# A vision tower on one core: four edits to its patch stage and to the place of two small matrices' powers

## The chip, the cores and the metric

The kernel runs on one core of one Trainium2 chip. The metric is the device time of one execution in microseconds (us). Three runs of the kernel before took 324.05, 324.23 and 325.01 us: median 324.23. Engines: PE is TensorE, DVE VectorE, ACT ScalarE, POOL GpSimd, SP SyncE. Transfers are issued on two queues here, SyncE's (q1 in the profile) and ScalarE's (q10), and run on the core's 16 DMA engines.

## The reference, cut to what matters

Sixteen images of 3 x 96 x 96 become 36 patches of 768 numbers each; with the class token an image has 37 tokens of 256, 592 in all. Two layers follow: attention and a mixture of experts, then an iterated attention with 16 x 16 matrices `Wlq`, `Wlk`, `Wlv` and a quantised feed-forward. The change touches the patch stage:

```
patches = x.reshape(B, C, h, P, w, P).transpose(0, 2, 4, 3, 5, 1).reshape(B, h*w, P*P*C)
y = layernorm(patches) * ln1_w + ln1_b
y = einsum('bnp,pd->bnd', y, lin_w) + lin_b
y = layernorm(y) * ln2_w + ln2_b
y = concatenate([cls_token, y], axis=1) + pos_embedding[:, :n + 1]
```

and, in the second layer's attention, in three iterations, `ql = qcur @ Wlq.T + blq`, `kl = kcur @ Wlk.T + blk`, `vl = vcur @ Wlv.T + blv` on every head, with `kcur, vcur = kl, vl` and `qcur` raised by each output. The kernel puts products of these small matrices (their powers) into the projections once.

## The kernel before, in words

Everything is fp32 and stays in the on-chip memory. Tokens lie in five tiles of 128 rows (`TT = 5`, the last of 80). The program of each engine is written out by hand, in order; engines wait for each other by semaphores. TensorE's eight banks are handed out in rotation in the order of one list, `fills()`: the n-th fill waits until the (n-8)-th has been emptied by the engine named beside it, and all engines count through the same list (`fill`, `full`, `take`, `empty`, `emptied`).

The patch stage, in TensorE's order:

- `ln`: after six matmuls on constants (`keep_awake`) TensorE transposes the rows of `ln1_w` and `ln1_b` (`ln_rows`, L1712); ScalarE copies them to `ln_cols` (L694).
- `ad`: `table` has 37 rows, the position embedding and seven selector columns. VectorE (`make_table`, L1015 to L1026) waits for three transfers (L663 to L665: positions, class token and `ln2_b`, the last two broadcast to 37 rows), adds the class token to row 0 and the bias to the others, and fills the selectors. Five products with `token_all` (for each of 640 token rows a 1 in the row of its position, made by GpSimd at L569) give the addend of every token; ScalarE copies them (L697).
- `channel(c)`: GpSimd (L579) and ScalarE (L684) copy the windows of an image's channel into patches, TensorE transposes them (L1729), ScalarE writes `patT` (L691).
- `cs`: the column sums of `lin_w` weighted by `ln1_w` and `ln1_b`, four chains of six products with `lin_w` as the stationary side and 2 moving columns; then `mr` and `cr`, the sums as rows on all partitions by transposes of a broadcast column (L1744). ScalarE makes `mean_row` (L703).
- VectorE computes the channel statistics from the images (L1068) and centres the six chunks of `lin_w` with `ln_cols` and `mean_row` (`centred_weights`, L1072), chunks 0 to 3 before the statistics of channel 2, 4 and 5 after the aggregates (L1083); then `c_row` (L1090), which empties the bank of `cr`.
- `y`: the embedding of tiles 0 and 1, chunk by chunk (L1775), after `channel(2)`; then the rates `rt`, tiles 2, 3 and 4. VectorE applies the second normalisation and adds the addend (L1125 to L1148).

Then `small_matrices`, the turned weights of the first attention, and `pw`, two fills of three products (`powers`), which ScalarE copies to `wlT` (L716); `turn` transposes the normalised tokens xn (L1840) into `xT` (L740) for the projections (L1865). The powers' users, `composed_weights` (`wc`), come on TensorE after the first attention, near 111 us; ScalarE scales and copies them (L720), in its order `q`, 1, 2, then the root of the variances for the next layer norm (L672), then 3. SyncE's queue issues the images (L480), `lin_w` (L483) and some thirty further transfers without waiting.

Of the kernel before, what the change touches and what calls it, by code (L numbers as in the profile page):

```python
# [84 lines left out]
POOL_WINDOWS = 4  # L85

# [3 lines left out]
def fills():  # L90
# [4 lines left out]
    f = [(("ln",), "act")]  # L95
    f.extend((("ad", t), "act") for t in range(TT))
# [15 lines left out]
    f.extend((("pw", n), "act") for n in range(2))  # L112
# [15 lines left out]
    f.extend((("wc", n), "act") for n in ("q", 1, 2, 3))  # L128
# [76 lines left out]
def build(nc, i, out):  # L205

    with ExitStack() as ctx:
# [89 lines left out]
        col_sums = cut(cur, 4)  # L297
# [18 lines left out]
        r_lin, r_ln2w, r_ln2b = (sqr_all[:, n * D:(n + 1) * D] for n in range(3))  # L316
        rsd_all = sb("rsd", P, NR * CF)
        rsd = rsd_all[:, :].rearrange("p (n t) -> p n t", n=NR)
        token_all = rsd_all[0:T, 0:NP]
        token_of = rsd_all[0:T, 0:NT].rearrange("p (b t) -> p b t", t=T)  # L320
# [4 lines left out]
        table = probs_all[0:T, 0:DA]  # L325
        r_cls = probs_all[0:T, 2 * D:3 * D]
# [80 lines left out]
        weights_centred = sem("weights_centred")  # L407
        attn_cleared = sem("attn_cleared")
# [123 lines left out]
        def _(pool):  # L532
# [35 lines left out]
            link(pool.memset(token_all[:, NT:NP], 0.0))  # L568
            pool.tensor_copy(token_of, ident[0:T, 0:T].unsqueeze(1).to_broadcast([T, B, T])).then_inc(consts_ready, 1)  # L569
# [78 lines left out]
        def _(act):  # L648
# [44 lines left out]
            b = take(act, ("ln",))  # L693
            empty(act.copy(ln_cols.rearrange("p c v k -> p (c v k)"), b[:, 0:4 * NC]))  # L694
            for t in range(TT):
                b = take(act, ("ad", t))
                empty(act.copy(addend[:, t, :], b[:, 0:DA]))  # L697
            windows(0)
            channel(0)
            b = take(act, ("cs",))  # L700
            empty(act.copy(col_sums, b[:, 0:4]))
# [44 lines left out]
            for n in range(2):  # L746
                powers(n)
# [57 lines left out]
            for n in ("q", 1, 2):  # L805
                composed_weights(n)
# [174 lines left out]
        def _(dve):  # L981
# [33 lines left out]
            def make_table():  # L1015

                dve.wait_ge(pos_in, 48)
                dve.tensor_reduce(table[:, D + 1:DA], ident[0:T, 1:T].rearrange("p (g w) -> p w g", g=NG), AX.X, ALU.add)  # L1018
                dve.tensor_scalar(first[:, 1:2], ident[0:T, 0:1], -1.0, 1.0, ALU.mult, ALU.add)
                link(dve.tensor_copy(first[:, 0:1], ident[0:T, 0:1]))  # L1020
                link(dve.scalar_tensor_tensor(out=table[:, 0:D], in0=r_cls, scalar=first[:, 0:1], in1=table[:, 0:D],
                                              op0=ALU.mult, op1=ALU.add))
                dve.tensor_copy(table[:, D:D + 1], first[:, 1:2])
                link(dve.scalar_tensor_tensor(out=table[:, 0:D], in0=r_ln2b[0:T, :], scalar=first[:, 1:2],
# [54 lines left out]
            for k in range(4):  # L1079
                centred_weights(k)  # L1080
# [1158 lines left out]
```

## Time and profile before

| | |
|---|---|
| median of three runs | 324.23 us |
| profiled execution, its own time | 322.2 us |
| its span | 320.5 us |
| TensorE busy | 264.7 us (83%), 2221 matmuls |
| VectorE busy | 201.6 us (63%) |
| ScalarE busy | 100.4 us (31%) |
| GpSimd busy | 45.0 us (14%) |

The span is what the views divide; the rest of the execution's time lies around it. Busy matmul time overlaps, since matmuls are pipelined. In the page's picture of 40 slices of 8 us, TensorE's row begins 403969: busy 40% of the first slice, under 10% of the second, 30% of the third, then 90% or more with one slice of 60%. The row PEclk gives the granted clock in tenths, 9 for nine tenths or more.

### The profile page before, as it was taken

Reading aid. Unit: us, or ns where it says so; the run is one execution under the profiler, and the core shown is the slowest. Engines: PE = TensorE matmul, PEld = TensorE weight load, DVE = VectorE, ACT = ScalarE, POOL = GpSimd, SP = SyncE. Lnnn points to the kernel's source line nnn. Section 1 sums busy time; section 2 is a strip of 40 time slices with the busy share of each in tenths; the row PEclk is TensorE's granted clock in tenths of the full one; section 3 lists DMA queues with packets and bytes.
Section 4 is the critical chain, followed back from the end, with each engine's and each line's share of the span. In section 5 each row is a group of like instructions: output and inputs, shape, how many; then the busy total and the mean of one; then the engine's idle time right before and its main releaser. Section 6 shows DMA issues by size and latency. Waiting matters only on the chain.

```text
span 320.5 us, 5617 instructions
## 1 busy us (share of the span) xinstructions
PE 264.7 (83%) x2221; PEld 218.8 (68%) x2221; DVE 201.6 (63%) x485; ACT 100.4 (31%) x238; POOL 45.0 (14%) x88
## 2 busy tenths in 40 slices
PE   4039699678987989999999998998868899937496
PEld 3028688578977757777787798876646677717484
DVE  1051608953683536889788962786788846997931
ACT  1004610333224154211111253476330533917000
POOL 7140000020053000000000000679400000000000
PEclk9999979879557999999999986999999999987789
DMA  7919500500000043000000000000000000000011
GB/s 205 221 22 314 169 2 1 164 3 2 4 0 2 4 149 146 2 0 0 0 2 1 0 2 1 2 3 0 4 0 3 0 0 2 0 0 0 1 35 43
DMA packets 14524, 12.10 MB, mean 38 GB/s; under 512 B 2975, under 2 KB 13954, under 8 KB 14498
## 3 DMA queue, kind: packets, MB, share of 16 engines
q1 hardware_dynamic: 14376, 11.62, 12.3%
q8 instruction: 18, 0.29, 0.4%
q10 hardware_dynamic: 122, 0.12, 0.1%
q14 instruction: 8, 0.07, 0.1%
HBM read 11.13 MB, written 0.61 MB: 37 GB/s over the span
## 4 chain that ended last, share of the span: by engine, by line
PE 66%; DVE 18%; ACT 6%; DMA 5%; issue 3%; ACTq 1%; DVEq 0%
PE bank L1702 47%; DMA sqr<-in_L_tok_ln_b 5%; PE bank L2206 5%; PE bank L1865 3%; PE bank L1898 2%; DVE part L1546 2%; PE bank L1775 2%; PE bank L1929 2%; DVE big L1610 1%; DVE keys_n L1591 1%; PE bank L1840 1%; PE bank L1973 1%; DVE big L1644 1%; ACT xT L740 1%; PE bank L1729 1%
## 5 line engine op out<-in xcount | busy, mean ns | idle before, releaser
L1702 PE MATMUL bank<-xT,big 128*128 128x296 f32 (+1 forms) x192 | 45.7, 391 | 0.0
L1702 PEld LDWEIGHTS bank<-xT,big 128*128 128x128 f32 x192 | 34.3, 190 | 9.5 <-issue 0.2
L1702 PE MATMUL bank<-xT,fT 128*128 128x296 f32 (+12 forms) x96 | 24.6, 416 | 0.6 <-DVE xT L1567 0.6
L1702 PE MATMUL bank<-big,cur 128*128 128x256 f32 (+1 forms) x100 | 23.3, 381 | 0.7 <-DVE cur L1321 0.7
L822 ACT ACTIVATE cen<-bank 128x296 f32<-128x296 f32 x20 | 8.3, 418 | 46.4 <-PE bank L1702 40.7
L1697 PE MATMUL bank<-ident,ones 128*128 128x128 f32 x100 | 17.1, 340 | 6.2 <-POOL rsd L569 4.4
L1702 PEld LDWEIGHTS bank<-xT,fT 128*128 128x128 f32 x96 | 17.2, 191 | 7.1 <-issue 2.1
L1702 PEld LDWEIGHTS bank<-big,cur 128*128 128x128 f32 (+1 forms) x100 | 18.0, 182 | 4.9 <-DVE cur L1321 1.5
L1697 PEld LDWEIGHTS bank<-ident,ones 128*128 128x128 f32 x100 | 16.4, 253 | 6.6 <-POOL rsd L569 4.4
L1334 DVE SCALAR_TENSOR_TENSOR h<-bank,route,h 128x256 f32<-128x256 f32 (+1 forms) x40 | 17.0, 478 | 2.8 <-PE bank L1702 2.8
L624 POOL TENSOR_SCALAR big<-keys_n,k_w 128x256 f32<-128x256 f32 x24 | 17.5, 750 | 6.4 <-DVE keys_n L1425 6.4
L1546 DVE TENSOR_REDUCE part<-big 128x1 f32<-128x296 f32 (+2 forms) x18 | 13.1, 731 | 6.3 <-ACT big L958 6.3
L1702 PE MATMUL bank<-probs,rsd 37*128 37x263 f32 x10 | 4.7, 658 | 13.4 <-DVE first L1026 13.4
L2206 PE MATMUL bank<-fT,big 128*128 128x256 f32 (+1 forms) x60 | 15.2, 419 | 0.6 <-DVE big L1543 0.6
L2206 PEld LDWEIGHTS bank<-fT,big 128*128 128x128 f32 (+1 forms) x60 | 12.2, 206 | 3.4 <-DVE big L1543 0.8
L1702 PEld LDWEIGHTS bank<-probs,rsd 37*128 37x128 f32 x10 | 3.2, 327 | 14.4 <-DVE first L1026 13.5
L616 POOL COPY cur<-xT 128x256 f32<-128x256 f32 x2 | 0.8, 404 | 80.9 <-ACT xT L742 80.9
L1321 DVE TENSOR_TENSOR cur<-cen,bank 128x296 f32<-128x296 f32 x20 | 9.1, 461 | 4.8 <-PE bank L1702 4.4
L1702 PE MATMUL bank<-wT_o,att 128*128 128x256 f32 (+1 forms) x40 | 9.3, 383 | 1.5 <-DVE att L1502 0.9
L606 POOL TENSOR_TENSOR big<-big,row_sum 128x370 f32<-128x370 f32 x8 | 6.2, 813 | 24.8 <-DVE row_sum L1217 24.8
L1702 PEld LDWEIGHTS bank<-wT_o,att 128*128 128x128 f32 (+1 forms) x40 | 7.0, 182 | 3.1 <-DVE att L1502 1.3
L1018 DVE TENSOR_REDUCE probs<-ident 37x6 f32<-37x36 f32 x1 | 0.2, 208 | 14.2 <-DMA sqr<-in_L_tok_ln_b 14.2
(312 smaller groups left out, 540.2 us busy)
## 6 DMA issues: line engine op xcount, KB each, us to landing
big<-in_x SPq DMA_DIRECT2D x3, 576.0 KB, 11.8
big<-in_L_ffn_w_gate SPq DMA_DIRECT2D x2, 512.0 KB, 6.5
big<-in_L_ffn_w_up SPq DMA_DIRECT2D x2, 512.0 KB, 6.7
big<-in_L_ffn_w_down SPq DMA_DIRECT2D x1, 1024.0 KB, 5.5
small<-in_L_tok_lin_w SPq DMA_DIRECT2D x3, 256.0 KB, 5.5
small<-in_L_ffn_w_gate SPq DMA_DIRECT2D x1, 768.0 KB, 4.6
small<-in_L_ffn_w_up SPq DMA_DIRECT2D x1, 768.0 KB, 6.8
small<-in_L_ffn_w_down SPq DMA_DIRECT2D x1, 768.0 KB, 8.1
```

The source lines that it names most:

```text
L624: ins = pool.tensor_scalar(fkeys[a - 1][:, u, :, n, :], keys, k_w[:, a - 1, n:n + 1], 1.0, ALU.mult, ALU.mult)
L822: empty(act.activation(silu[:, c, :], b[:, 0:HP], ACT.Silu))
L1321: empty(dve.tensor_tensor(hid[:, e % 3, c * HP:(c + 1) * HP], silu[:, c, :], b[:, 0:HP], ALU.mult))
L1334: ins = dve.scalar_tensor_tensor(out=v, in0=src, scalar=route[0:n, t, e:e + 1], in1=v, op0=ALU.mult, op1=ALU.add)
L1546: return dve.tensor_reduce(part[:, n:n + 1], v, AX.X, ALU.max, apply_absolute_value=True)
L1697: pe.matmul(b[:, 0:P], ones[:, :], ident[:, :], start=True, stop=True)
L1702: ins = pe.matmul(out_, a_, b_, start=(n == 0), stop=(n == len(pairs) - 1))
L1775: ins = pe.matmul(bs_[t][:, 0:D], patT[:, k, t * P:(t + 1) * P], lin_w[:, k, :], start=(k == 0), stop=(k == PK - 1))
L1865: ins = pe.matmul(b[32 * j:32 * j + m, at_:at_ + 4 * T].rearrange("p (u c) -> p u c", u=2), w(k), xq[:, k, :, 2 * j * T:2 * (j + 1) * T], ...
L1898: ins = pe.matmul(bs_[j][:, (2 * t + s) * T:(2 * t + s + 1) * T], qT[rows, row:row + P], kT[rows, u, s * T:(s + 1) * T], start=True, stop= ...
L1929: ins = pe.matmul(b[32 * q:32 * q + 32, m * 2 * T:(m + 1) * 2 * T].rearrange("p (i t) -> p i t", i=2), vals[0:G3, 3 * u + g, s, h_, :], by ...
L2206: ins = pe.matmul(b[0:rows, 0:D], gate[:, o * NT + t * P:o * NT + t * P + rows], fT[2][:, o, :], start=(o == 0), stop=(o == FC - 1))
```

## The change

- ScalarE's first transfers: the positions in 32 rows and 5 rows, the class token and `ln2_b` as one row each, all to `table`, which now has 39 rows (`TR = T + 2`); then the two of `ln1`. The broadcasts are gone.
- GpSimd builds `token_all` with 39 rows: token 0 of an image selects row 0 and row 37, the others their position and row 38. So the products add class token and bias. `make_table` keeps two instructions and waits for no transfer; TensorE waits for the four transfers before the first product, after `keep_awake` with 4.
- The five products come before the transposes of `ln1`, and ScalarE's copies accordingly.
- The column sums are one chain of six products with `ln_cols` as the stationary side (2 columns) and `lin_w` moving (256 columns), two rows as result; `mr` and `cr` are products of a selector over two partitions with these rows.
- Chunks 4 and 5 of `lin_w` are centred by GpSimd, in two instructions each, after its windows; its clearing of three regions follows.
- Chunks 0 and 1 of the embedding of tiles 0 and 1 come before `channel(2)`, the rest after it; their banks are opened ahead of the list's order.
- The powers move from before the first `turn` to between the composed weights, on TensorE and on ScalarE.

```diff
-    f = [(("ln",), "act")]
-    f.extend((("ad", t), "act") for t in range(TT))
+    f = [(("ad", t), "act") for t in range(TT)]
+    f.append((("ln",), "act"))
...
-    f.extend((("pw", n), "act") for n in range(2))
...
-    f.extend((("wc", n), "act") for n in ("q", 1, 2, 3))
+    f.extend((key, "act") for key in (("pw", 0), ("wc", "q"), ("pw", 1), ("wc", 1), ("wc", 2), ("wc", 3)))
...
-            link(pool.memset(token_all[:, NT:NP], 0.0))
-            pool.tensor_copy(token_of, ident[0:T, 0:T].unsqueeze(1).to_broadcast([T, B, T])).then_inc(consts_ready, 1)
+            pool.memset(token_all[:, NT:NP], 0.0)
+            pool.tensor_tensor(row_of[:, 0:1], ident[0:TR, 0:1], ident[0:TR, T:T + 1], ALU.add)
+            link(pool.tensor_tensor(row_of[:, 1:T], ident[0:TR, 1:T], ident[0:TR, T + 1:TR].to_broadcast([TR, T - 1]), ALU.add))
+            pool.tensor_copy(token_of, row_of.unsqueeze(1).to_broadcast([TR, B, T])).then_inc(consts_ready, 1)
...
+            emptied(pool, ("ln",))
+            emptied(pool, ("mr",))
             pool.wait_ge(windows_pool, NC * POOL_WINDOWS)
+            for k in range(DVE_CHUNKS, PK):
+                v = lin_w[:, k, :]
+                link(pool.tensor_scalar(v, v, ln_cols[:, k // 2, 0, k % 2:k % 2 + 1], 1.0, ALU.mult, ALU.mult))
+                pool.tensor_tensor(v, v, mean_row, ALU.subtract).then_inc(weights_centred_pool, 1)
             pool.memset(fprobsT[:, :, :], 0.0)
...
+            for lo, hi in ((0, 32), (32, T)):
+                act.dma_start(table[lo:hi, 0:D], i["L0_tok_pos_embedding"][0, lo:hi, :]).then_inc(pos_in, 16)
+            act.dma_start(table[T:T + 1, 0:D], i["L0_tok_cls_token"][0, 0:1, :]).then_inc(pos_in, 16)
+            act.dma_start(table[T + 1:TR, 0:D], i["L0_tok_ln2_b"].unsqueeze(0)).then_inc(pos_in, 16)
             for n, name in enumerate(("L0_tok_ln1_w", "L0_tok_ln1_b")):
                 act.dma_start(ln_rows[2 * n:2 * n + 2, :], i[name].rearrange("(k m) -> k m", k=2)).then_inc(ln_in, 16)
-            act.dma_start(table[:, 0:D], i["L0_tok_pos_embedding"][0, :, :]).then_inc(pos_in, 16)
-            act.dma_start(r_cls, i["L0_tok_cls_token"][0, 0, :].partition_broadcast(T)).then_inc(pos_in, 16)
-            act.dma_start(r_ln2b[0:T, :], i["L0_tok_ln2_b"].partition_broadcast(T)).then_inc(pos_in, 16)
...
-            empty(act.copy(col_sums, b[:, 0:4]))
+            empty(act.copy(col_sums, b[0:2, 0:D]))
...
-                dve.wait_ge(pos_in, 48)
-                dve.tensor_reduce(table[:, D + 1:DA], ident[0:T, 1:T].rearrange("p (g w) -> p w g", g=NG), AX.X, ALU.add)
...
+                dve.tensor_reduce(table[:, D + 1:DA], ident[0:TR, 1:T].rearrange("p (g w) -> p w g", g=NG), AX.X, ALU.add)
+                dve.tensor_copy(table[:, D:D + 1], ident[0:TR, T + 1:TR]).then_inc(table_ready, 1)
...
-            for n in range(2):
-                ins = product(b[:, 2 * n:2 * n + 2], [(lin_w[:, k, n * P:(n + 1) * P], ln_cols[:, k // 2, :, k % 2]) for k in range(PK)])
-            full(ins)
+            full(product(b[0:2, 0:D], [(ln_cols[:, k // 2, :, k % 2], lin_w[:, k, :]) for k in range(PK)]))
...
-                for n in range(2):
-                    ins = pe.transpose(b[:, n * P:(n + 1) * P], col_sums[:, 2 * n + v:2 * n + v + 1].to_broadcast([P, P]), ident[:, :])
-                full(ins)
+                full(product(b[:, 0:D], [(ident[0:2, v:v + 1].to_broadcast([2, P]), col_sums)]))
             channel(1)
+            first_banks = [opened(("y", t)) for t in range(2)]
...
+            embedding_of_first(range(2))
             channel(2)
+            for t in range(2):
+                fill(("y", t))
+            embedding_of_first(range(2, PK))
...
+            emptied(pe, ("bl",))
+            powers(0)
             composed_weights("q", "q1", q_)
-            for n in range(2):
-                emptied(pe, ("pw", n))
-            for a in (1, 2, 3):
-                composed_weights(a, "k1", KEY_POWER[a - 1])
+            emptied(pe, ("pw", 0))
+            powers(1)
+            composed_weights(1, "k1", KEY_POWER[0])
+            composed_weights(2, "k1", KEY_POWER[1])
+            emptied(pe, ("pw", 1))
+            composed_weights(3, "k1", KEY_POWER[2])
```

`embedding_of_first(ks)` holds the old loop over chunks for tiles 0 and 1, for the chunks `ks`, and waits for `weights_centred` (chunks 0 to 3) or `weights_centred_pool` (4 and 5). `opened` waits for a bank as `fill` does but does not count the fill.

## Rows read from the trace of the kernel before

**Rows 1.** The chain of waits in order: start us, us, what.
```profile
2.47 17.11 DMA sqr<-in_L_tok_ln_b
...
21.25 4.75 PE bank L1702 x10
...
28.21 4.98 PE bank L1702 x24
...
34.16 0.39 ACT cur L703
```

**Rows 2.** Timeline to 32 us: start, us, engine, line, operation [idle before].
```profile
4.44 2.93 PE L1697 MATMUL bank<-ident,ones 128*128 128x128 f32 x12 [4.44 <-POOL rsd L569]
...
7.30 0.50 PE L1712 MATMUL bank<-ident,cur 4*128 4x4 f32 x3
...
15.17 2.96 POOL L579 COPY fT<-big 96x256 f32<-96x256 f32 x8 [7.69 <-DMA big<-in_x]
...
19.60 0.21 DVE L1018 TENSOR_REDUCE probs<-ident 37x6 f32<-37x36 f32 x1 [14.21 <-DMA sqr<-in_L_tok_ln_b]
...
25.93 2.29 PE L1729 MATMUL bank<-ident,fT 96*128 96x96 f32 x12
```

**Rows 3.** The queues' transfers from 3 to 12 us.
```profile
DMA packets 1242, 2.50 MB, mean 278 GB/s; under 512 B 94, under 2 KB 984, under 8 KB 1242
...
q10 hardware_dynamic: 70, 0.07, 3.5%
```

**Rows 4.** Timeline from 32 us: centring, ScalarE's copies of a channel, the constant row.
```profile
34.58 1.67 DVE L1072 SCALAR_TENSOR_TENSOR small<-small,cur 128x256 f32<-128x256 f32 x4 [9.46 <-ACT cur L703]
35.06 2.29 ACT L691 COPY big<-bank 128x288 f32<-128x288 f32 x4
...
39.60 0.41 DVE L1090 TENSOR_TENSOR cur<-bank,sqr 128x256 f32<-128x256 f32 x1
```

**Rows 5.** Timeline from 62 us: the powers and the first turn.
```profile
62.59 1.69 DVE L1043 TENSOR_SCALAR xn<-h,mv,rstd 128x256 f32<-128x256 f32 x5
...
64.95 1.65 PE L1702 MATMUL bank<-wlT 128*128 128x128 f32 x6 [0.57 <-ACT wlT L716]
...
67.25 1.52 PE L1840 MATMUL bank<-ident,xn 128*128 128x128 f32 x10
...
69.84 0.71 PE L1865 MATMUL bank<-xT,wkvT 128*32 128x148 f32 x16 [1.07 <-ACT xT L740]
70.34 8.36 PE L1865 MATMUL bank<-xT,wT_q 128*32 128x148 f32 x256
```

**Rows 6.** Windows of L1775, then of L1729: us, PE, PEld, granted clock, DMA.
```profile
41.17:43.73 2.56, 2.56 (x7) 2.02 (x6) 0.50 0.02 6
44.24:46.83 2.59, 2.59 (x13) 2.28 (x12) 1.00 0.00 0
...
34.33:36.73 2.40, 2.39 (x15) 2.40 (x16) 1.00 0.83 279
37.87:38.11 0.24, 0.24 (x3) 0.24 (x3) 1.00 0.00 0
```

**Rows 7.** Timeline from 96 us: the composed weights and the root.
```profile
111.16 3.73 PE L1702 MATMUL bank<-wlT,small 128*128 128x128 f32 x32
...
112.79 0.45 DVE L1038 BATCH_NORM_AGGREGATE mv<-st 128x2 f32<-128x6 f32 x5
...
114.53 0.29 ACT L672 ACTIVATE var<-mv,eps_c 128x5 f32<-128x5 f32 x1
```

**Rows 8.** GpSimd's groups by form: busy us, mean ns, idle before.
```profile
L640 POOL TENSOR_TENSOR keys_n<-cen,rsd 128x256 f32<-128x256 f32 x4 | 3.0, 738 | 0.6 <-ACT rsd L853 0.6
...
L568 POOL MEMSET rsd<- 37x48 f32 x1 | 0.1, 131 | 0.0
```

**Rows 9.** Windows of all engines: us, PE, PEld, DVE, ACT, POOL, clock, DMA.
```profile
64.40:67.80 3.40, 2.85 (x13) 2.85 (x14) 2.31 (x10) 0.96 (x2) 2.23 (x3) 0.50 0.00 0
67.80:71.20 3.40, 2.33 (x53) 2.12 (x55) 1.81 (x8) 1.54 (x6) 0.00 (x0) 1.00 0.01 2
```

More of the change, by code:

```diff
@@ L85 @@
 POOL_WINDOWS = 4
+DVE_CHUNKS = 4
+TR = T + 2
 def fills():
@@ L697, in _ @@
                 empty(act.copy(addend[:, t, :], b[:, 0:DA]))
+            b = take(act, ("ln",))
+            empty(act.copy(ln_cols.rearrange("p c v k -> p (c v k)"), b[:, 0:4 * NC]))
             windows(0)
@@ L1015, in make_table @@
             def make_table():
-                dve.wait_ge(pos_in, 48)
-                dve.tensor_reduce(table[:, D + 1:DA], ident[0:T, 1:T].rearrange("p (g w) -> p w g", g=NG), AX.X, ALU.add)
[L1019 to L1024, printed above, removed]
-                                              in1=table[:, 0:D], op0=ALU.mult, op1=ALU.add))
-                dve.tensor_copy(first[:, 0:1], ident[0:T, 0:1]).then_inc(table_ready, 1)
+                dve.tensor_reduce(table[:, D + 1:DA], ident[0:TR, 1:T].rearrange("p (g w) -> p w g", g=NG), AX.X, ALU.add)
+                dve.tensor_copy(table[:, D:D + 1], ident[0:TR, T + 1:TR]).then_inc(table_ready, 1)
             def statistics(ts):
@@ L1078, in _ @@
             emptied(dve, ("ln",))
-            for k in range(4):
+            for k in range(DVE_CHUNKS):
                 centred_weights(k)
@@ L1083, in _, with constant_row @@
                 ins = dve.bn_aggr(mv[0:96, w, :], st[0:96, 3 * w:3 * w + 3, :].rearrange("p a b -> p (a b)"))
-            def rest_of_weights():
-                for k in range(4, PK):
-                    centred_weights(k)
+            def constant_row():
                 dve.wait_ge(norm_rows_in, 32)
@@ L1705, in _ @@
             pe.wait_ge(consts_ready, N_CONSTS)
+            for t in range(TT):
+                b = fill(("ad", t))
+                if t == 0:
+                    keep_awake(b, 4)
+                    pe.wait_ge(table_ready, 1)
+                    pe.wait_ge(pos_in, 64)
+                full(product(b[:, 0:DA], [(token_all[:, t * P:(t + 1) * P], table)]))
             b = fill(("ln",))
-            keep_awake(b, 6)
             pe.wait_ge(ln_in, 32)
@@ L1713, in _ @@
             full(ins)
-            pe.wait_ge(table_ready, 1)
-            for t in range(TT):
-                b = fill(("ad", t))
-                full(product(b[:, 0:DA], [(token_all[:, t * P:(t + 1) * P], table)]))
             def channel(c):
@@ L1767, in small_matrices @@
                 full(product(b[:, 0:2 * NH], [(bq8.rearrange("p n d -> p (n d)"), ident[0:2 * NH, 0:2 * NH])]))
-            bs_ = [fill(("y", t)) for t in range(2)]
-            for k in range(PK):
-                pe.wait_ge(weights_centred, k + 1)
-                for g in range(2):
-                    emptied(pe, ("xp", k, g))
-                for t in range(2):
-                    ins = pe.matmul(bs_[t][:, 0:D], patT[:, k, t * P:(t + 1) * P], lin_w[:, k, :], start=(k == 0), stop=(k == PK - 1))
-                    if k == PK - 1:
-                        full(ins)
             def embedding(ts):
@@ L1812, in _, with powers @@
             q_, k_, v_, nk, nv = range(5)
-            emptied(pe, ("bl",))
-            for n in range(2):
-                if n:
-                    emptied(pe, ("pw", 0))
+            def powers(n):
                 b = fill(("pw", n))
@@ L1974, in weight_turned @@
                 full(ins)
+            emptied(pe, ("bl",))
+            powers(0)
             composed_weights("q", "q1", q_)
-            for n in range(2):
-                emptied(pe, ("pw", n))
-            for a in (1, 2, 3):
-                composed_weights(a, "k1", KEY_POWER[a - 1])
+            emptied(pe, ("pw", 0))
+            powers(1)
+            composed_weights(1, "k1", KEY_POWER[0])
+            composed_weights(2, "k1", KEY_POWER[1])
+            emptied(pe, ("pw", 1))
+            composed_weights(3, "k1", KEY_POWER[2])
             turn(1, 2)
```

41 lines of the change are left out of this document (28 added, 13 removed).

## The prediction, made before the run

> **What bounds the kernel now.** I read the chain of waits in order of time first, because the change touches two places, the first 47 us and the small matrices' powers near 63 us and 111 us. After the issues of the small transfers the chain waits 17.11 us for one transfer, the broadcast of `L0_tok_ln2_b` into 37 rows; then come the table on VectorE, five products of 37 rows, the transposes of channel 0, the column sums, two rows, centring, and the embedding [rows 1]. The timeline shows what stands behind it: TensorE has nothing from 7.8 to 21.25 us; VectorE waits 14.21 us for that transfer and its channel statistics queue behind it [rows 2]. From 47 to 62 us TensorE and VectorE work as before in both kernels; from 62.7 to 66.6 us TensorE does the powers while xn is being made [rows 5]. At 111 us the order reverses: the composed weights on TensorE hold back ScalarE, whose root of the variance waits behind them although VectorE's aggregates end at 113.2 [rows 7].
>
> **Why the small transfers are late.** Image 1 releases GpSimd only at 15.17 [rows 2], yet in 3 to 12 us the queues moved 2.50 MB, as much as all three images (576 KB each) and the patch weights (3 of 256 KB); ScalarE's queue moved 70 of its 122 packets [rows 3]. So one of the 16 engines is late, and ScalarE's queue is not limited by bytes (0.07 MB in 9 us). My reading: the three transfers of 37 rows (111 KB) run on one engine, one row at a time between that engine's image rows. That both delays the table and holds back images 1 and 2.
> The Trainium skill, "DMA: Bandwidth & Descriptors", section "Why a DMA increments its semaphore by 16 and not by 1", says a transfer uses the largest number of engines up to 16 that divides its slowest dimension: 1 for 37 rows, 16 for 32, 5 for 5. By that rule the trace agrees, and the page gives no time for it; the sum below does not need it.
>
> **Part 1, the transfers.** After: 32 + 5 rows of positions, one row of class token, one of bias, then the two of `ln1`: six issues in place of five, one more of about 0.4 us on ScalarE, which is idle. Data falls from 111 rows to 39. When are four of them in? At best before keep_awake ends (6.5 us, below), when nothing is lost. At worst, image 0 lands at 6.06 and the transfers share with the patch weights after it: 9 us. I take 6.6 us: the last `ln1` row, issued second, was in by 7.3 when TensorE asked [rows 2].
>
> **Part 2, the chain from 4.4 us.** GpSimd gets two small tensor_tensor before the token pattern: 0.13 us each by a small memset, 0.74 at most by 128x256 elements [rows 8]; 39x1 and 39x36 are near the memset; I take 0.35 with the link: TensorE starts at 4.8 (bounds 4.7 to 5.9).
> keep_awake 4: 8 instructions at 0.213 (12 took 2.56 start to start [rows 2]) = 1.7, to 6.5. VectorE's three constants end 1 us after the start, the table's two remaining instructions take 0.35: ready at 6.2, hidden under keep_awake. The four removed VectorE instructions and the wait go off the chain with it, and statistics 0 follow at once, 1 when its image lands: both (4.0 us) are done by 17.2 even if image 1 still comes at 15.2, so they cost nothing.
> Five products: 4.7 as before (21.25 to 25.93 [rows 1, 2]), from 6.6 to 11.3. Transposes of `ln1` 0.35, channel 0 2.0, of which 12 x 0.160 are transposes; ScalarE's copy of ln_cols now stands before its windows, 0.2 that the first half of the transposes hides: to 13.6. The patch weights, in by 13 at the latest by [rows 3], don't delay.
> Column sums: 12 instructions of 256 columns instead of 24 of 2. The 24 took 4.98 [rows 1], 0.213 each start to start. A 256-column instruction costs 0.427 at half clock and 0.216 at full: in the embedding 2.56 us hold 6 and 2.59 us hold 12 of them, by the weight loads, which count no instruction twice [rows 6]. So 12 x 0.427 + 0.2 = 5.3, to 18.9: no gain at half clock, 2.5 us at full.
> The copy of the sums is 2 x 256 instead of 128 x 4: 0.39 by mr's own copy [rows 1], some 0.2 more. mr: 2 instructions of 256 columns instead of 2 of 128: +0.43. From sums to centring 34.58 - 33.19 = 1.4 [rows 1, 4] becomes 2.0. Centring begins at **20.9 instead of 34.6: -13.7**.
>
> **Part 3, centring and embedding.** VectorE keeps 4 chunks (1.67). GpSimd does 2, each of two instructions of 128x256 at 0.74 [rows 8], and a link: 3.1 together, to 24.0; needed after channel 2, at 28 or later: hidden, with 4 us of cover. The memsets pushed behind it (2 us) are not asked for before the attention. VectorE frees the bank of `cr` 40.0 - 34.6 = 5.4 after centring begins, less two chunks 0.8 [rows 4]: at 25.5.
> TensorE: `cr` to 21.1, channel 1's transposes 12 x 0.160 to 23.1 (ScalarE's windows come at 21.8), then, new, chunks 0 and 1 of the first two tiles while ScalarE copies channel 1: 8 x 0.427 = 3.4 to 26.5 (at full clock 1.7, then channel 2 waits for `cr`: a gain of 1.0 only). Channel 2 to 27.6, its last of four copies (2.29 for four [rows 4], from 26.9) at 29.2; chunks 2 and 3 1.7 to 29.3, 4 and 5 1.7: **31.2 instead of 47.27: -16.1**. The extra 2.4 over part 2 is the embedding's first third pulled ahead, and the old run's half-clock stretch at 40 to 44 us [rows 6] not met. The rest up to xn is the same work on TensorE and VectorE.
>
> **Part 4, the powers.** Removed before the turn: from xn's first tile (62.59 + 0.33 = 62.9) TensorE could transpose; now it starts at 67.25 [rows 5]. After: transposes of 5 tiles, 10 x 0.213 at half clock, 65.1, last copy 65.6; before, the q projections began at 69.84: **-4.2**. Added at 111 us: 12 instructions of 128x128 at 3.73/32 = 0.117 = 1.4 us, in front of the second weight's copy, behind which the root waits [rows 7]. Their two copies fit between ScalarE's. **+1.4**, bounds 1.4 to 2.5 (both round trips waited out, 0.57 each as before [rows 5]). Clock: the old powers kept TensorE at work through 64.4 to 67.8, and the granted clock was 1.00 from 67.8, just before 272 instructions of projections [rows 5, 9]. Without them TensorE stands idle to 62.9; some 2.6 us of the projections run at half clock: +1.3 (bounds 0 and 3.4). Net **-1.5**.
> The Trainium skill, "TensorE: Matmul & The Clock Gate", Part 1, speaks against this move in the same sense (an idle window throttles the array); no sum here rests on it.
>
> **Sum.** 320.5 - 16.1 - 1.5 = 302.9 span; profiled time 322.2 is 1.7 above its span: 304.6. The median of the runs is 2.0 above the profiled run: 306.6. One upward chance (next paragraph) pulls it: I say **306.0**. About 0.3% (1 us) is what this kernel's measurement can tell from no change.
>
> **Rivals.**
> *TensorE's clock rises early.* The page prints a granted clock of 1.00 for the first 37 us, but 15 transposes of 96 columns take 2.40 us at 34.3 and 3 take 0.24 at 37.9: 0.160 against 0.082 each. So the clock was at 1.2 GHz until 37, though TensorE was busy from 21.25 [rows 6]: 37-row products and 2-column products did not raise it, 128-row transposes did. The new column sums stream 256 columns from 128 rows; if that counts, half of the sums (-1.4), mr and cr (-0.6) and the next transposes run at full clock, then VectorE's 4.6 us from mr to cr bounds: 302 to 303. For: the work is denser. Against: only two columns of the array are filled. 0.30.
> [...]
> *The clock stays low a window or two longer* in the embedding: each 16 instructions of 256 columns +3.4; 308 to 313. 0.14.
> *The transfers do not come earlier* (the change does not do what it says): the table's rows at 19.6 still, products to 24.4, channel 0 26.9, sums 32.2, centring 34.2: -0.4, -2.4 and -1.5: 324.2 - 4.3 = 320. Against: no byte limit. 0.04.
> *Slower:* TensorE never gets its full clock before the attention. Then the 16 late and 36 further embedding instructions cost 52 x 0.211 = 11.0 more and the projections another 8.4 - 1.3 = 7.1; transposes and small products 1.5: +19.6 against -17.6, so 326. It decides from half clock reaching beyond the projections' middle. For: half clock for 16 busy us in this trace. Against: it was full from 43.9 through the same embedding [rows 6]. 0.02.
> The forecast itself has 0.48; 0.02 is left for what I don't see.
>
> **Range and chances.** The forecast's own range is 304 to 309. With the clock cases: **301.5 to 311**. Faster 0.97, same 0.01, slower 0.02.
>
> **What would show it.** Image 1 releases GpSimd near 11 us; the 37-row products (now 39) start near 6.6; 12 column-sum instructions 0.427 apart (or 0.216 from some point); centring on VectorE near 20.9; four chunks there, two on GpSimd; last of chunk 5 near 31; no gap for `cr` over 1 us; xT's last copy 50 us into the run; the composed weights' stretch 1.4 longer. Wrong if the products start after 9, if GpSimd's chunks end after channel 2's copies, or if the q projections take over 12 us.

## The result, and the profile after

| | kernel before | changed kernel |
|---|---|---|
| median of its runs in the comparison | 324.14 us (4 runs, 323.09 to 325.01) | 304.14 us (4 runs, 303.68 to 306.71) |
| ratio, with 95% interval | | 0.940 [0.934, 0.946] |
| profiled execution, its own time | 322.2 us | 306.71 us |
| its span | 320.5 us | 304.9 us |

The forecast was 306.0 us, range 301.5 to 311. The profiled execution of the changed kernel is the longest of its four; the other three have spans of 301.9 to 302.4 us. A profile taken later of the same kernel (`a2_changed_again`, below) has 302.2 us, and both are used. The later one is the usual case: of ten executions of the changed kernel eight took 303.62 to 304.17 us with a mean granted clock of 0.926 to 0.927, and two took 306.36 and 306.71 us with 0.905. Ratios leave out executions that lie over 1.5% above the fastest of their kernel: one of the kernel with three edits together and two of the last kernel below.

The changed kernel's page, its span, its engines and the row of the granted clock:
```profile
span 304.9 us, 5589 instructions
...
PE 265.3 (87%) x2205; PEld 215.1 (71%) x2205; DVE 200.4 (66%) x478; ACT 100.6 (33%) x238; POOL 48.2 (16%) x94
...
PEclk9998975965599999999999759999999999977689
```
TensorE's and VectorE's busy time is what it was (264.7 and 201.6 us): the kernel does nearly the same work and waits less. The clock row of this execution has more low digits in the first 80 us than before.

The chain of waits of the changed kernel (start us, us, what), which answers to [rows 1]:
```profile
4.80 2.07 PE bank L1704 x8
6.88 4.68 PE bank L1709 x10
...
14.10 4.94 PE bank L1709 x12
...
22.36 3.48 PE bank L1763 x8
...
26.83 3.48 PE bank L1763 x16
30.31 8.90 PE bank L1709 x46
```
No transfer stands in it: the 17.11 us of [rows 1] are gone, and from 4.8 us the chain is TensorE's nearly throughout.

Its timeline to 32 us, against [rows 2] and [rows 4]:
```profile
6.81 4.75 PE L1709 MATMUL bank<-probs,rsd 39*128 39x263 f32 x10
...
11.10 1.43 POOL L583 COPY fT<-big 96x256 f32<-96x256 f32 x4 [3.30 <-DMA big<-in_x]
...
14.03 4.99 PE L1709 MATMUL bank<-small,cur 128*2 128x256 f32 x12
...
20.62 2.58 DVE L1076 SCALAR_TENSOR_TENSOR small<-small,cur 128x256 f32<-128x256 f32 x4 [7.50 <-ACT cur L714]
...
25.83 0.36 DVE L1092 TENSOR_TENSOR cur<-bank,sqr 128x256 f32<-128x256 f32 x1
```
The products with the table follow on TensorE's own work, image 1 releases GpSimd at 11.10 instead of 15.17, and centring begins at 20.62 instead of 34.58.

The queues' transfers from 3 to 12 us, against [rows 3]:
```profile
DMA packets 1236, 2.54 MB, mean 282 GB/s; under 512 B 107, under 2 KB 967, under 8 KB 1236
...
q10 hardware_dynamic: 22, 0.01, 0.6%
```
The whole rate is the same (282 against 278 GB/s). ScalarE's queue has 22 packets in these 9 us instead of 70.

Its timeline at the projections and at the composed weights, against [rows 5] and [rows 7]:
```profile
49.98 9.60 PE L1878 MATMUL bank<-xT,wT_q 128*32 128x148 f32 x256
...
60.75 1.50 PE L1911 MATMUL bank<-kT,qT 16*128 16x37 f32 x45 [1.17 <-ACT qT L766]
...
92.12 0.83 PE L1709 MATMUL bank<-wlT 128*128 128x128 f32 x6
...
94.35 2.84 PE L1709 MATMUL bank<-wlT,small 128*128 128x128 f32 x24
...
96.83 0.29 ACT L683 ACTIVATE var<-mv,eps_c 128x5 f32<-128x5 f32 x1
```
256 projections take 9.60 us where they took 8.36, and the powers (2 x 6) now stand in front of the root.

Late in the run, the chain of the kernel before, and then that of the changed one (from the product with the gate weights on):
```profile
193.59 13.48 PE bank L1702 x132
...
302.72 15.18 PE bank L2206 x60
```
```profile
100.07 2.33 PE bank L1709 x8
...
176.56 14.44 PE bank L1709 x132
...
286.61 15.71 PE bank L2223 x60
```
So at the 132 products and at the last 60 the changed kernel is ahead by 17.0 and by 16.1 us.

How far it is ahead, stage by stage (start before minus start after; the last column is how far the later profile of the same kernel is ahead):

| stage | before | after | ahead | later profile |
|---|---|---|---|---|
| centring | 34.58 | 20.62 | 14.0 | 15.3 |
| embedding of two tiles ends | 47.43 | 30.31 | 17.1 | 18.6 |
| projections begin | 69.84 | 49.02 | 20.8 | 22.9 |
| first scores | 79.84 | 60.75 | 19.1 | 21.5 |
| product with the gate weights | 117.77 | 100.07 | 17.7 | 20.5 |
| the 132 products of layer two | 193.59 | 176.56 | 17.0 | 19.8 |
| the last 60 products | 302.72 | 286.61 | 16.1 | 18.9 |
| end of the span | 320.5 | 304.9 | 15.6 | 18.3 |

### The profile page after: what moved, and what is told of

Read it like the earlier page. It is cut to its first block, busy times and chain, and to the rows that moved or that the text cites. A ratio compares the mean times of both kernels' runs of the same rounds, so it can differ in the third digit from the quotient of the medians.

```text
span 304.9 us, 5589 instructions
## 1 busy us (share of the span) xinstructions
PE 265.3 (87%) x2205; PEld 215.1 (71%) x2205; DVE 200.4 (66%) x478; ACT 100.6 (33%) x238; POOL 48.2 (16%) x94
## 4 chain that ended last, share of the span: by engine, by line
PE 71%; DVE 17%; ACT 6%; issue 3%; POOL 1%; ACTq 0%; DVEq 0%; POOLq 0%
PE bank L1709 49%; PE bank L2223 5%; PE bank L1878 3%; DVE part L1548 2%; PE bank L1911 2%; PE bank L1763 2%; PE bank L1942 2%; PE bank L1853 2%; DVE big L1612 1%; DVE keys_n L1593 1%; PE bank L1737 1%; PE bank L1986 1%; PE bank L1704 1%; DVE big L1646 1%; ACT big L983 1%
## 5 line engine op out<-in xcount | busy, mean ns | idle before, releaser
L1704 PE MATMUL bank<-ident,ones 128*128 128x128 f32 x96 | 16.2, 336 | 6.7 <-POOL rsd L573 4.8
L1704 PEld LDWEIGHTS bank<-ident,ones 128*128 128x128 f32 x96 | 15.2, 246 | 7.1 <-POOL rsd L573 4.8
L1548 DVE TENSOR_REDUCE part<-big 128x1 f32<-128x296 f32 (+2 forms) x18 | 13.1, 731 | 6.3 <-ACT big L970 6.3
L1853 PE MATMUL bank<-ident,xn 128*128 128x128 f32 x40 | 8.5, 359 | 3.5 <-DVE xn L1047 3.3
L1853 PEld LDWEIGHTS bank<-ident,xn 128*128 128x128 f32 x40 | 6.2, 186 | 5.4 <-DVE xn L1047 2.7
L1047 DVE TENSOR_SCALAR xn<-h,mv,rstd 128x256 f32<-128x256 f32 x20 | 7.0, 405 | 4.0 <-ACT rstd L684 4.0
L1878 PE MATMUL bank<-xT,wT_q 128*32 128x148 f32 (+1 forms) x256 | 9.6, 316 | 0.0
```

Source lines behind the costliest of these rows:

```text
L1047: dve.tensor_scalar(xn[:, t, :], h[:, t, :], mv[:, t, 0:1], rstd[:, t:t + 1], ALU.subtract, ALU.mult).then_inc(xn_ready, 1)
L1548: return dve.tensor_reduce(part[:, n:n + 1], v, AX.X, ALU.max, apply_absolute_value=True)
L1704: pe.matmul(b[:, 0:P], ones[:, :], ident[:, :], start=True, stop=True)
L1853: ins = pe.transpose(b[:, at_:at_ + P], xn[:, t, k * P:(k + 1) * P], ident[:, :])
L1878: ins = pe.matmul(b[32 * j:32 * j + m, at_:at_ + 4 * T].rearrange("p (u c) -> p u c", u=2), w(k), xq[:, k, :, 2 * j * T:2 * (j + 1) * T], ...
```

## The experiments

Unless the text says otherwise a kernel is the changed kernel with one edit. The kernel before was run again beside each group of experiments: medians 322.94 (7 runs), 322.71 (10) and 322.4 us (11). Ratios are to those. My theory: the transfers give more than half of the gain, the reordered embedding the rest, and TensorE's clock takes back what the powers' move brings. Theory A, of the clock: the table's products, which fill 39 of 128 rows, do not raise it here; its rival is that they do as much for it as any others that keep TensorE busy as long.

**The changed kernel again** (no edit).

> The changed kernel itself, timed again beside the three others: 304.1, ratio 0.940. It is the level against which single microseconds of the others are read.

303.96 us (303.62 to 306.36), 0.944 [0.940, 0.948]. Its timeline:
```profile
14.03 3.64 PE L1709 MATMUL bank<-small,cur 128*2 128x256 f32 x12
...
19.26 2.58 DVE L1076 SCALAR_TENSOR_TENSOR small<-small,cur 128x256 f32<-128x256 f32 x4 [6.09 <-ACT cur L714]
...
25.20 3.65 PE L1763 MATMUL bank<-small,big 128*128 128x256 f32 x16
...
46.99 1.21 PE L1878 MATMUL bank<-xT,wkvT 128*32 128x148 f32 x16 [0.74 <-ACT xT L751]
```
The same twelve products take 3.64 us, not 4.99: the full clock came at 15.9 us, not at 18.6. By the projections this execution is 2.0 us ahead of the first profile, and it ends 2.7 us shorter. One kernel lands on either side of the forecast's step "sums at half clock". Here TensorE waits 1.17 us for the bank of `cr`, where the forecast expected no gap over 1 us, and still ends the embedding of two tiles 1.5 us earlier (28.84). The Trainium skill, "TensorE: Matmul & The Clock Gate", Part 1, says that how many matmuls run at the low clock at a start varies from run to run; these two profiles agree.

**The kernel before, with only the transfers split.**

```diff
+            for lo, hi in ((0, 32), (32, T)):
+                act.dma_start(table[lo:hi, 0:D], i["L0_tok_pos_embedding"][0, lo:hi, :]).then_inc(pos_in, 16)
+                act.dma_start(r_cls[lo:hi, :], ...partition_broadcast(hi - lo)).then_inc(pos_in, 16)
+                act.dma_start(r_ln2b[lo:hi, :], ...partition_broadcast(hi - lo)).then_inc(pos_in, 16)
```

> The kernel before, with each of the three transfers of 37 rows split into one of 32 and one of 5; all else as before. My theory (37 rows run on one engine, row after row, and hold back the images there): the last one is in near 8 us instead of 19.6, image 1 near 11 instead of 15.2, the table's products begin near 9.8 instead of 21.25 and centring near 23 instead of 34.6; 311 to 314 us. The rival (the queue of ScalarE simply waits behind the images and patch weights, however its rows are cut): table still after 15 us, image 1 still near 15, 320 us or more.

313.63 us (312.0 to 314.37), 0.971 [0.967, 0.975]. Its timeline:
```profile
9.81 0.21 DVE L1019 TENSOR_REDUCE probs<-ident 37x6 f32<-37x36 f32 x1 [4.42 <-DMA sqr<-in_L_tok_ln_b]
...
11.89 1.43 POOL L579 COPY fT<-big 96x256 f32<-96x256 f32 x4 [3.95 <-DMA big<-in_x]
...
24.79 1.67 DVE L1073 SCALAR_TENSOR_TENSOR small<-small,cur 128x256 f32<-128x256 f32 x4 [9.47 <-ACT cur L704]
```
The same bytes, in rows of 32 and 5, release the table at 9.81 us instead of 19.60 and image 1 at 11.89 instead of 15.17; centring comes at 24.79 instead of 34.58. That is half of the change's gain (9.3 us by the medians of this group, 322.94 to 313.63, against 18.8 to the changed kernel's 304.14). The last row landed some 2 us later than I had expected; why is not shown. The other half lies in two places of the profiles. At centring this kernel is 4.2 us behind the changed one (24.79 against 20.62): its table's products start at 11.46, behind the last broadcast row and VectorE's work on the table, and not at 6.81. No run takes that edit (class token and bias by the product) alone. At the end of the two tiles' embedding it is 8.7 us behind (39.01 against 30.31), so another 4.5 us lie between, in the order of the embedding and in the clock, which rises only at 36.5 us here; undoing that order alone costs 5.1 us, below.

**The positions in one transfer of 37 rows** (one execution).

```diff
-            for lo, hi in ((0, 32), (32, T)):
+            for lo, hi in ((0, T),):
```

> The changed kernel with the positions as one transfer of 37 rows instead of 32 and 5. Theory (37 rows run on one engine, one row between two of the images' or the patch weights'): the table's products start near 8 instead of 6.8 us, image 1 lands about 1.7 us later than 11.05 (37 rows on its slowest engine), and the end comes 1 us later: 305. Rival (rows of 37 are spread as well as 32): products at 6.8, image 1 at 11, 304.0.

303.82 us, span 302.1. Its timeline:
```profile
7.35 4.72 PE L1709 MATMUL bank<-probs,rsd 39*128 39x263 f32 x10 [0.47 <-DMA probs<-in_L_tok_ln_b]
...
12.49 1.43 POOL L583 COPY fT<-big 96x256 f32<-96x256 f32 x4 [3.99 <-DMA big<-in_x]
```
Products 0.5 us later and image 1 1.4 us later than in the first profile of the changed kernel. That is little beside the spread: in the eight profiles here with the positions in 32 + 5 rows and no clearing before them, the products start at 6.79 to 6.81 us in seven and at 7.20 in one, and image 1 comes between 10.62 and 12.16. So one third of the rows delays it by at most 1.9 us, and whether at all is not shown. The sums start 0.5 us later too (14.54), but the clock rose at 18.4 and centring (20.77) is as in the first profile. The Trainium skill, "DMA: Bandwidth & Descriptors", section "Why a DMA increments its semaphore by 16 and not by 1", puts 37 rows on one engine and 32 rows on 16; the kernel above, whose table came at 9.81 and not at 19.60, agrees with it in direction. No view here shows the engine of a packet.

**The powers back before the projections.**

```diff
+            powers(0)
+            powers(1)
...
-            powers(0)
-            emptied(pe, ("pw", 0))
-            powers(1)
-            emptied(pe, ("pw", 1))
```

> The changed kernel with the powers back before the first turn. The forecast's part 4 (powers moved: -4.2 at 63 us, +1.4 at 111, +1.3 of half clock): 1.5 us slower than the changed kernel, 305.6. The changed kernel's trace, where TensorE's clock stays half until 52.7 instead of 50, suggests less: -3.9 + 1.4 + 1.7, so 0.8 slower. If the powers' place gives nothing: the same as 304.1, with projections of 8.9 us instead of 10.6.

304.9 us (303.94 to 305.42), 0.945 [0.942, 0.948]. Its chain, and then one row of its timeline:
```profile
53.35 8.80 PE bank L1884 x272
...
63.26 2.44 PE bank L1917 x80
...
99.68 2.33 PE bank L1710 x8
...
284.77 14.87 PE bank L2224 x60
```
```profile
96.43 0.29 ACT L684 ACTIVATE var<-mv,eps_c 128x5 f32<-128x5 f32 x1
```
This profile and the first one of the changed kernel can be laid side by side: the clock rose at 18.5 and 18.6 us, and the two tiles' embedding ends at 30.32 and 30.31. The projections begin 4.3 us later than in the changed kernel, but take 8.80 us and not 10.60, so the first scores are 2.5 us later; 33 us on, with no powers in front of it, the root is 0.4 us earlier, and so is the gate product (99.68 against 100.07). On the way there the clock was at 1.2 GHz from 66.3 to 83.3 us here and from 63.0 to 83.5 in the changed kernel. By the medians the changed kernel is 0.8 to 0.9 us faster (304.14 and 303.96 against 304.9), and the ratios' intervals overlap. So the sign of what moving the powers gives is not shown, and the 1.5 us of the forecast aren't either.

**The column sums in their old form.**

```diff
-            full(product(b[0:2, 0:D], [(ln_cols[:, k // 2, :, k % 2], lin_w[:, k, :]) for k in range(PK)]))
+            for n in range(2):
+                ins = product(b[:, 2 * n:2 * n + 2], [(lin_w[:, k, n * P:(n + 1) * P], ln_cols[:, k // 2, :, k % 2]) for k in range(PK)])
```

> The changed kernel with the column sums and the two rows as before (24 instructions of 2 moving columns, transposes of a broadcast column). Theory: 256 moving columns from 128 rows raised the clock at 18.6 us and 2 moving columns don't; with the old form the clock rises only after channel 1's transposes, near 25, so transposes of channel 1 take 1.9 us instead of 1.35 and chunks 0 and 1 3.4 us (they were at half clock in the changed kernel's trace too); the sums themselves cost the same 5.1 us, the copy is 0.2 shorter, mr 0.4 shorter: between 0.5 faster and 1.5 slower than 304.1. If the form doesn't touch the clock: full clock again from about 18.6 to 22.

304.54 us (303.36 to 305.42), 0.943 [0.939, 0.947]. Its timeline:
```profile
13.89 5.17 PE L1709 MATMUL bank<-cur,small 128*128 128x2 f32 x24
...
20.45 2.59 DVE L1076 SCALAR_TENSOR_TENSOR small<-small,cur 128x256 f32<-128x256 f32 x4 [6.27 <-ACT cur L714]
```
24 instructions of 2 columns take what 12 of 256 take at half clock. The full clock comes at 23.8 us, where all eight profiles with the new sums and 39-row products have it between 15.6 and 18.6. The form is worth nothing that the medians show (304.54 against 304.14 and 303.96 us).

**Channel 2 before the first two chunks.**

```diff
-            embedding_of_first(range(2))
             channel(2)
...
-            embedding_of_first(range(2, PK))
+            embedding_of_first(range(PK))
```

> The changed kernel with channel 2's transposes before all chunks of the embedding, as in the kernel before. Theory (chunks 0 and 1 fill the time in which channel 2 waits for ScalarE's copies and for the bank of the constant row): 24 instructions then start near 26.6 and end near 31.9 at full clock, 1.6 us later; with TensorE idle from 22.5 to 26 the clock may fall as at 40 us in the kernel before, another 1.7: 305.7 to 307.5. Rival (the early chunks only fill time that is lost anyway to ScalarE's copies of channel 2): 304.1.

309.02 us (308.66 to 309.58), 0.959 [0.956, 0.962]. Its timeline, then its windows (us, PE, PEld, DVE, ACT, POOL, clock, DMA):
```profile
25.65 0.74 PE L1737 MATMUL bank<-ident,fT 96*128 96x96 f32 x3 [1.95 <-DVE cur L1092]
...
26.18 7.78 PE L1763 MATMUL bank<-small,big 128*128 128x256 f32 x24
```
```profile
24.20:31.00 6.80, 5.35 (x15) 4.37 (x16) 1.36 (x9) 1.54 (x5) 0.91 (x2) 0.50 1.04 313
```
5.1 us slower, more than I expected. With nothing to multiply, TensorE waits 1.95 us for the bank of `cr`, and the clock is at 1.2 GHz from 24.2 to 31.0, over about half of the 24 products. Against the later profile of the changed kernel the products begin 1.0 us later (26.18 against 25.20), eight more of them are still to do (8 x 0.216 = 1.7), and the 24 take 2.4 us more than at full clock (7.6 against 24 x 0.216 = 5.2): together 5.1. So the clock is about half of it.

**All six chunks on VectorE.**

```diff
+                for k in range(DVE_CHUNKS, PK):
+                    centred_weights(k)
```

> The changed kernel with all six chunks centred by VectorE, 4 and 5 after the aggregates as before. Theory (GpSimd's share has 4 us of cover and buys nothing; VectorE's instructions are slowed by it: 4 took 2.58 us instead of 1.67): centring's first four take 1.67, the two more 0.8 before the constant row, so its bank is free at the same time within 0.2: 304.0 plus or minus 0.5. Rival (VectorE bounds there): 0.8 slower.

303.32 us (301.6 to 304.73), 0.940 [0.935, 0.945]. Its timeline:
```profile
19.67 1.67 DVE L1072 SCALAR_TENSOR_TENSOR small<-small,cur 128x256 f32<-128x256 f32 x4 [7.02 <-ACT cur L710]
...
24.70 0.41 DVE L1090 TENSOR_TENSOR cur<-bank,sqr 128x256 f32<-128x256 f32 x1
```
Four chunks take 1.67 us here, where GpSimd only clears regions beside them, and 2.58 where it centres its own two. `cr`'s bank is free 5.4 us after centring begins, against 5.6 in the changed kernel. What GpSimd takes over it takes back by slowing VectorE: no difference that the medians show.

**Seven matmuls on constants before the turn, in place of two.**

```diff
-            turn(0, 1, awake=2)
+            turn(0, 1, awake=7)
```

> The changed kernel with 7 instead of 2 matmuls on constants before the first turn; they end at 45.8 at half clock, when the first tile of xn comes (45.8). Theory (TensorE's idle 1.9 us there let its clock fall for the transposes and the first 3.7 us of the projections, which ate half of what moving the powers had given): projections of 272 instructions 8.9 instead of 10.6 us, 302.4. Rival (the window in which the clock is judged falls elsewhere in each execution, and the attention that follows runs at half clock anyway): no more than 0.5 faster.

302.33 us (299.34 to 303.65), 0.937 [0.933, 0.942]. Inconclusive: 1.6 us less by the medians, but the ratio's interval overlaps that of the changed kernel, and the profile shows no cause. Its projections:
```profile
47.81 9.18 PE L1878 MATMUL bank<-xT,wT_q 128*32 128x148 f32 x256
```
The clock was 0.50 from 46.3 to 49.7 us all the same. At the full clock seven matmuls last only half of what I had counted, and TensorE still stood idle for 1.38 us before the turn.

**The root before the powers' last users on ScalarE.**

```diff
+            inverse_root(P, slice(0, TT))
...
-            inverse_root(P, slice(0, TT))
```

> The changed kernel with ScalarE's root of the variances after the second powers' copy instead of after the second key weight's. Theory (the root waits for TensorE's composed weights, not for the variances, which are ready at 94.2): xn begins near 95.4 instead of 97.5, TensorE's transposes follow its last composed weight at 97.3 instead of 98.0, and ScalarE's copies can follow at once: 0.8 to 1.3 faster, 302.9 to 303.3. Rival (TensorE is the bound there): 304.1, with the root early and no other row moved.

302.04 us (300.93 to 303.04), 0.937 [0.934, 0.941]. Its timeline:
```profile
93.97 0.30 ACT L683 ACTIVATE var<-mv,eps_c 128x5 f32<-128x5 f32 x1
...
96.07 1.25 PE L1853 MATMUL bank<-ident,xn 128*128 128x128 f32 x10
```
From the attention's output products (12 instructions, at 88.50 us) to the gate product (98.02) it takes 9.52 us, against 10.61 in the later profile of the changed kernel (86.69 to 97.30): 1.1 us. By the medians it is 1.9 us, and the two ratios' intervals just touch; what the rest of it would be is not shown. The path there was ScalarE's order, as the prediction said of [rows 7]; but the last 24 products, from 93.39 to 96.2, then bound the transposes, so no more is to be had by this.

**The table's products over 128 rows** (the rows from 39 are zeros, cleared by VectorE).

```diff
-                full(product(b[:, 0:DA], [(token_all[:, t * P:(t + 1) * P], table)]))
+                full(product(b[:, 0:DA], [(token_rows[:, t * P:(t + 1) * P], table_rows)]))
```

> The changed kernel with the table's five products over 128 rows instead of 39: rows 39 to 127 of both sides are cleared by VectorE at the start and add zero; ScalarE's transfers wait for the clearing. Theory A (TensorE's activity counts filled rows, so products of 39 rows do not raise its clock): the clock is full before the column sums (near 14 us or earlier), these take 2.6 us instead of 5.1, centring begins 2.5 to 4 us earlier, 300 to 302 us. Theory B (what is streamed counts, or the clock rises only by chance of its phase): half clock through the column sums as now, 304.3 (0.3 later for the clearing).

300.88 us (298.83 to 302.75), 0.932 [0.926, 0.938]. Its timeline:
```profile
6.85 4.48 PE L1714 MATMUL bank<-probs,rsd 128*128 128x263 f32 x10
...
13.20 2.75 PE L1714 MATMUL bank<-small,cur 128*2 128x256 f32 x12
...
17.55 2.58 DVE L1081 SCALAR_TENSOR_TENSOR small<-small,cur 128x256 f32<-128x256 f32 x4 [4.51 <-ACT cur L717]
```
The same ten products of the same columns, now with zeros in the other rows, and the full clock comes at 11.0 us: the sums take 2.75 us for twelve and centring is 3.1 us earlier than in the first profile, 1.7 earlier than in the later one. The two kernels below have the same rows, and there it comes at 13.1 and 9.9 us. So three profiles with 128 rows have it between 9.9 and 13.1 us and eight with 39 rows between 15.6 and 18.6, and Theory A holds for this kernel: the 39-row products kept TensorE as busy (4.75 us) and did not raise the clock. The interval lies wholly below that of the later runs of the changed kernel (0.940 to 0.948) and overlaps that of the first four (0.934 to 0.946). The Trainium skill, "TensorE: Matmul & The Clock Gate", Part 1, has the clock set by how busy TensorE has been recently; with 39 filled rows the same busy time did not raise it, and the measurement decides.

**Three together:** 128 rows, seven matmuls, early root.

> The changed kernel with three edits together: table products over 128 rows, 7 matmuls on constants before the first turn, root early. If their gains add (3.1 by e9_rows_128, 1.6 by e7_awake_7, 1.9 by e8_root_early against the changed kernel's 304.0): 297.5 to 298.5. If the gain of the constants was a matter of the clock's phase: 299 to 299.5.

299.11 us (296.23 to 301.03), 0.925 [0.920, 0.930]. The sum of the three (3.1 + 1.6 + 1.9 us by their medians against the changed kernel's 303.96) would be 297.4. The median lies in the range of the second expectation (299 to 299.5), but the six executions spread over both, so which of the two holds is not shown. Its profile (span 299.3 us) is of its longest execution; there the clock is 0.50 from 57.4 to 77.9 us.

**The powers in TensorE's waits.** From the kernel above: each of the two fills of three products goes into one of TensorE's waits in the attention.

```diff
+        if not u:
+            f.append((("pw", 0), "act"))
+        if u:
+            f.append((("pw", 1), "act"))
...
-    f.extend((key, "act") for key in (("pw", 0), ("wc", "q"), ("pw", 1), ("wc", 1), ("wc", 2), ("wc", 3)))
+    f.extend((key, "act") for key in (("wc", "q"), ("wc", 1), ("wc", 2), ("wc", 3)))
```

> e10_three with the powers moved once more: the first set into TensorE's wait for ScalarE's copies of the first probabilities (2.7 us idle at 75.8 in the changed kernel), the second into its wait for the last heads (0.7 us), ScalarE's copies behind those it is waited for. Theory (near 92 us the powers cost TensorE 1.4 us on the path; in the gaps 0 and some 0.2): 1.2 faster than e10_three. Rival (ScalarE's copy of the first set delays the heads, or the bank order adds a wait): no faster.

295.4 us (293.05 to 298.18), 0.913 [0.907, 0.919]: faster than both kernels. Its timeline, and its clock row:
```profile
69.74 1.49 PE L1718 MATMUL bank<-wlT 128*128 128x128 f32 x6
...
80.26 0.94 PE L1718 MATMUL bank<-wlT 128*128 128x128 f32 x6
...
83.62 3.73 PE L1718 MATMUL bank<-wlT,small 128*128 128x128 f32 x32
...
85.74 0.30 ACT L690 ACTIVATE var<-mv,eps_c 128x5 f32<-128x5 f32 x1 [0.42 <-DVE mv L1049]
```
```profile
PEclk9999999956999999999999689999999999978689
```
The powers are gone from the path of the root, which again waits for VectorE's aggregates. I expected 1.2 us against the kernel above and measured 3.7. In the attention the clock is low from 57.7 to 71.4 us and between 9.9 and 57.7 there is no low stretch. The profile above is of that kernel's longest execution and can't be held against this one, but another thing can: in all nine profiles of other kernels whose low stretch in the attention is as long as this one's (13.7 us), the clock falls once more, 3.4 us later, for 3.4 us. Here it stays full, with the powers in two waits of TensorE. How much of the 3.7 us is the clock and how much the order was not separated.

## Why the prediction came out

**Part 1, right.** Forecast: products with the table from 6.6 us, image 1 near 11. Measured 6.81, on TensorE's own work, and 11.10. Splitting the same bytes alone (313.63 us) shows the cause: how the rows are cut into transfers, not the bytes. That 37 rows share one engine is a reading which the split agrees with; the trace doesn't show it.

**Part 2, right, with one term mis-sized that differs between executions.** TensorE starts at 4.80 (4.8), sums begin at 14.03 (13.6), centring at 20.62 (20.9). "No gain at half clock" held where the clock was low (4.99 us) and failed where it was full (3.64 us, in the later profile): the rival "TensorE's clock rises early" is, in part, what that execution did. The rival's 302 to 303 and the forecast's 306.0 lie on either side of the median, 304.14. By their mean clock, the late rise of the forecast belongs to two of ten executions and the earlier rise, part of the way to the rival, to eight.

**Part 3, the end right, two terms off.** VectorE's four chunks take 2.58 us, not 1.67: the cost of GpSimd beside it was missing. `cr` is free at 26.2, not 25.5. GpSimd ends at 23.8 (24.0), hidden as forecast. Chunks 0 and 1 take 3.48 us (3.4) and chunks 2 to 5 another 3.48 (1.7 and 1.7); the two tiles end at 30.3, not 31.2, since the early chunks began at 22.4 and not at 23.1: 17.1 us ahead instead of 16.1. That the chunks pulled ahead also keep the clock up was not in the working; it is 2.4 of the 5.1 us that channel 2 first lost.

**Part 4, a gain of 1.5 us that the runs don't show.** The projections begin 3.7 us further ahead than the embedding ended (4.2 forecast), take 1.7 us longer (1.3), and from the first scores to the gate product 1.4 us are lost (1.4). That is a net 0.6 against the kernel before. Against the kernel with the powers put back, which shares all else, it is +4.3, -1.8 and -2.9, so 0.4 us lost at the gate product. Of the 2.9, 1.3 lie behind the attention, where the powers now stand, and 1.6 in the attention, of which the sum had nothing: it counted half clock in the projections only, and the changed kernel's low stretch there is 20.5 us long where that kernel's is 17.1. The old place cost TensorE 4.2 us and bought the clock for the projections with it, as [rows 9] had it.

**What the sum did not have.** 320.5 - 17.1 - 0.6 = 302.8, the forecast's span of 302.9. The profiled span is 304.9: another 1.6 us goes between the gate product and the last 60 products, and 0.5 in these. The granted clock is 0.50 from 172.2 to 182.4 there, and before from 190.7 to 197.5: 132 products take 14.44 us instead of 13.48, the last 60 take 15.71 instead of 15.18. These are the same instructions, and nothing of the change touches them. The later profile pays the same: 20.5 us ahead at the gate product, 18.9 at the last 60. All 14 profiles together show what the 1.6 us are. From the gate product to the last 60 it is 184.7 to 185.1 us in the seven whose low stretch there lasts 6.8 us, and 186.4 to 186.6 in the seven where it lasts 10.2. The kernel before is in the first group and both profiles of the changed kernel are in the second, but the kernels with the positions in 37 rows, the powers put back, the early root and 128 rows are in the first (185.07, 185.09, 184.92 and 184.93 us), and none of these edits touches that part. So the 1.6 us are no price of the change's own instructions. The long stretch in the changed kernel's windows (columns as above):
```profile
172.20:182.40 10.20, 9.28 (x43) 8.82 (x43) 1.11 (x3) 3.14 (x11) 0.75 (x2) 0.50 0.01 2
```
That the sum's 302.9 lies near the spans of the usual executions (301.8 to 302.4) is in part luck: in the later profile the earlier clock puts the changed kernel 20.5 us ahead at the gate product where the sum had 17.6, and the second layer takes 2.2 of that back. By the medians the change gave 20.0 us, 2.4 more than the sum. The 306.0 had 2.0 us added for the kernel before's median above its own profile, and the changed kernel's profile lay above its median, by 2.6: a correction taken from one execution carries its scatter into the forecast. The rivals on the other side (late transfers, half clock to the attention) did not occur.

Left open: why the low stretch of the second layer lasts 6.8 us in some profiles and 10.2 in others, and what of the gain the table's products with class token and bias have by themselves.

## What to carry to other kernels

A small transfer can be late and hold back a large one: look at how its rows are cut, and not only at its bytes. Three transfers of 37 rows cost 9.3 us here that the same rows in 32 + 5 did not. Before a step is counted as gained on TensorE, ask what it did for the clock of what follows; work that filled a wait was worth more here than its own duration (the chunks ahead of channel 2: 5.1 us for 3.5 or less), and moving work out of a wait was worth less (the powers: 4.3 us at the projections, nothing sure at the end). Two executions of one kernel can differ by more than a small edit, so a forecast term that depends on the clock needs both levels.

## What the runs showed of the hardware

- Products that fill 39 of 128 rows kept TensorE busy for 4.75 us and left the clock at 1.2 GHz; with zeros in the other rows it was 2.4 GHz from 11.0, 13.1 and 9.9 us in three profiles, against 15.6 to 18.6 in eight.
- The record of the granted clock begins at its first change; ahead of it the page prints 1.00, while twelve products of 256 columns take 4.99 us (1.2 GHz) and not 2.75.
- VectorE's 128x256 operation with two inputs takes 0.42 us beside GpSimd's clearing of regions (four in 1.67) and 0.65 beside GpSimd's operations of that size on the other chunks (four in 2.58).
- One kernel took 303.6 to 304.2 us in eight executions (mean clock 0.926 to 0.927) and 306.4 to 306.7 in two (0.905).
- The same second-layer work took 184.7 to 185.1 us with 6.8 us at 1.2 GHz in it and 186.4 to 186.6 with 10.2.
